# The lead-in moved wholly into the first block of an attention kernel, with low parts subtracted by GpSimd

## The reference

```
q_in = x Wq; Q = [q_in, conv3(q_in)] Wqproj            (K likewise, V = x Wv), 16 heads of 16
tau, delta = sigmoid(pointwise(gelu(depthwise_conv3(x))))   one row per head each
S = Q K^T / 4 * tau[query] + delta[key]; out = softmax(S) V
x = layernorm(x + out Wout)
x = layernorm(x + quantised_linear(x))
```

## Time and profile before

| what | us |
|---|---|
| median of 3 runs (lowest, highest) | 1694.66 (1692.73, 1697.91) |
| the profiled execution | 1700.33 |
| its span | 1698.5 |
| TensorE busy (share of the span) | 1642.5 (97%) |
| VectorE busy | 1538.2 (91%) |
| ScalarE busy | 1322.7 (78%) |
| GpSimd busy | 74.6 (4%) |
| its mean granted clock of TensorE, as a share of full | 0.981 |

### The profile page before, as it was taken

How to read it: one execution, slowest core, us unless ns; L and a number is a source line. 1 busy time by engine, 2 the same in 40 slices (tenths; PEclk the granted TensorE clock), 3 DMA queues, 4 the chain that set the end, 5 groups by cost and what they waited for, 6 DMA issues and landing times.

```text
span 1698.5 us, 33654 instructions
## 1 busy us (share of the span) xinstructions
PE 1642.5 (97%) x13972; PEld 745.1 (44%) x13978; DVE 1538.2 (91%) x1638; ACT 1322.7 (78%) x2389; POOL 74.6 (4%) x133
## 2 busy tenths in 40 slices
PE   8999989999999999999999999999999999998977
PEld 7677754333333333333333333333333333334466
DVE  5588977999999999999999999999999999985797
ACT  3688723888888888888888888888888888885534
POOL 3000003000000000000000000000000000001110
PEclk9899997999999999999999999999999999999998
DMA  3376436000600060006002400322050000002232
GB/s 111 91 191 171 123 91 95 9 8 8 76 16 8 8 84 8 8 9 83 8 14 30 66 8 8 51 44 61 29 71 21 8 8 8 8 8 86 82 101 75
DMA packets 46961, 84.73 MB, mean 50 GB/s; under 512 B 9116, under 2 KB 21020, under 8 KB 44092
## 3 DMA queue, kind: packets, MB, share of 16 engines
q1 hardware_dynamic: 44952, 82.49, 22.6%
q10 hardware_dynamic: 1856, 0.09, 0.1%
HBM read 51.36 MB, written 30.67 MB: 48 GB/s over the span
## 4 chain that ended last, share of the span: by engine, by line
PE 62%; DVE 21%; ACT 1%; issue 1%; ACTq 0%; POOL 0%; DVEq 0%
PE ps L846 26%; PE ps L833 20%; DVE mx L218 17%; PE ps L208 11%; PE ps L869 1%; PE ps L914 1%; PE ps L867 1%; PE ps L820 0%; DVE stats L1059 0%; DVE work L1094 0%; DVE work L1093 0%; ACT e L989 0%; DVE work L1085 0%; DVE small L1080 0%; DVE scr L1089 0%
## 5 line engine op out<-in xcount | busy, mean ns | idle before, releaser
L218 DVE TENSOR_REDUCE mx<-ps 128x2 f32<-128x1024 f32 x1024 | 1230.4, 1223 | 60.6 <-PE ps L208 51.2
L989 ACT ACTIVATE e<-ps 128x512 f32<-128x512 f32 x2048 | 1110.3, 596 | 210.5 <-PE ps L833 170.4
L846 PE MATMUL ps<-e,v_grp 128*32 128x256 f32 x8192 | 657.7, 393 | 0.2 <-issue 0.2
L833 PE MATMUL ps<-q,k 52*128 52x512 f32 x2048 | 525.3, 499 | 4.0 <-ACT e L989 4.0
L208 PE MATMUL ps<-k,q 50*128 50x512 f32 x2048 | 420.8, 404 | 11.1 <-DVE mx L218 6.5
L833 PEld LDWEIGHTS ps<-q,k 52*128 52x128 f32 x2048 | 199.4, 184 | 430.8 <-ACT e L989 400.0
L846 PEld LDWEIGHTS ps<-e,v_grp 128*32 128x32 f32 x8192 | 162.1, 108 | 359.2 <-issue 202.4
L208 PEld LDWEIGHTS ps<-k,q 50*128 50x128 f32 x2048 | 198.9, 188 | 39.7 <-DVE mx L218 31.0
L608 PE MATMUL ps<-x_p,m_p 128*128 128x512 f32 x576 | 143.1, 405 | 0.0
L608 PEld LDWEIGHTS ps<-x_p,m_p 128*128 128x128 f32 x576 | 109.1, 193 | 31.0 <-issue 6.5
L440 DVE SCALAR_TENSOR_TENSOR hid<-x_c,dw_w,hid 128x512 f32<-128x512 f32 x128 | 88.5, 746 | 13.2 <-ACT hid L382 13.2
(11 more groups left out here) (127 smaller groups left out, 621.8 us busy)
## 6 DMA issues: line engine op xcount, KB each, us to landing
k<-k_parts SPq DMA_DIRECT2D x42, 256.0 KB
q<-q_parts SPq DMA_DIRECT2D x42, 256.0 KB
k_parts<-k_sp SPq DMA_DIRECT2D x16, 512.0 KB, 5.1
q_parts<-q_sp SPq DMA_DIRECT2D x16, 512.0 KB, 4.6
att<-ev SPq DMA_DIRECT2D x32, 256.0 KB
x_c<-in_x_t SPq DMA_DIRECT2D x8, 514.0 KB, 6.4
tau_r<-tau_rows SPq DMA_DIRECT2D x16, 256.0 KB
x_in<-in_x SPq DMA_DIRECT2D x8, 512.0 KB, 3.7
```

The lines of the kernel that those rows point to most:

```text
L218: nc.vector.tensor_reduce(mx[:, j % 2, :, jh, qt, kc], ps[:, b0:b0 + 2, :], AX.X, ALU.max).then_inc(s_free, 1)
L833: nc.tensor.matmul(ps[:, st_bank(n), :], k_set[r, g % 2, jh, kt * P:(kt + 1) * P], q_set[r, g % 2, jh, lo:lo + CH], start=True, stop=True) ...
L846: last = nc.tensor.matmul(ps[32 * h:32 * (h + 1), 0, PVW * part:PVW * (part + 1)], v_grp[:, kt, h, :], e[:, x % E_BUFS, h * CH + PVW * par ...
L989: nc.scalar.activation(e[:, x % E_BUFS, h * CH:(h + 1) * CH], ps[:, st_bank(n), :], ACT.Exp).then_inc(e_ready, 1)
```

## The change

The lead-in at the start of the second block goes, with its unused products. The first block now issues 42 items in steps 2 to 7 over 15 places in a step, some of them inside a projection (after products 6, 12 and 18). The loop begins with item 42 in place of 45. Query block 0 takes its units by key chunk, so that a unit only needs the chunks loaded so far. The row maxima of query block 0 are split, transposed and stored in step 7. The low parts of x, delta and q are subtracted by GpSimd. The second half of the values of chunk 0 goes to bank 5. ScalarE's table for the exponential is loaded by an extra instruction at the end of the first block. SyncE waits for the stores of k, q and delta at the start of the second block, and for the group load before the one that it issues.

```diff
-        lead_in = items.index((1, LEAD))
+        def place_of(j, u):
+            if j == 0:
+                return u % (HH * TT) // HH, u % HH, u // (HH * TT)
+            return u // (HH * NQ), u // NQ % HH, u % NQ
 ...
+            qt, jh, kc = place_of(j, u)
+            if j == 0 and (qt, jh) == (0, 0):
+                pe.wait_ge(group_loaded, 16 * GROUP_DMAS * (kc + 1))
+            if u == 0 and j % NQ == 0 and j > 0:
                 pe.wait_ge(group_loaded, loads_of(g + 1))
 ...
-        V_BANK, TD_BANK = 2, 3
+        v_bank = lambda n, v: 5 if (n, v) == (0, 1) else 2
+        TD_BANK = 3
-        PRE_STEP = {4: (0, 0, 0, 0, 0, 0, 2), 5: (0, 0, 1, 1, 1, 1, 1), 6: (0, 0, 1, 1, 1, 1, 1), 7: (2, 2, 2, 2, 2, 2, 4)}
+        ONE_EACH = lambda *places: [int(p in places) for p in range(15)]
+        PRE_STEP = {2: ONE_EACH(6, 9, 10, 13, 14)} | {n: ONE_EACH(5, 6, 9, 10, 13, 14) for n in range(3, 7)} | {7: [1] * 13 + [0, 0]}
+        DVE_PLACES = ((0, 1, 2), (3, 4, 5), (6,), (7, 8, 9), (10,), (11, 12, 13), (14,))
 ...
+                        if n > 1:
+                            sp.wait_ge(group_loaded, 16 * GROUP_DMAS * (n - 1))
                         group_load(sp, 0, group_loaded, slice((n - 1) * CH, n * CH))
 ...
+                    if n == NCHUNK - 1:
+                        rows_store(sp, 0)
 ...
+                def split_low(n):
+                    pool.wait_ge(x_high, n + 1)
+                    low(nc.gpsimd, x_p[:, n % 2, 1], x_c[:, n % 2], x_p[:, n % 2, 0]).then_inc(x_ready, 1)
+                    pool.wait_ge(x_ready, n + 1)
 ...
+                for n in range(NCHUNK):
+                    if n + 1 < NCHUNK:
+                        split_low(n + 1)
+                    if n == NCHUNK - 1:
+                        split_max(pool, 0)
+                        pool.wait_ge(nm_ready, 1)
+                    pool.wait_ge(d_high, n + 1)
+                    low(nc.gpsimd, d_sp[32:32 + H, 1], td[32:32 + H], d_sp[32:32 + H, 0]).then_inc(d_split, 1)
+                    pool.wait_ge(d_split, n + 1)
+                    for o in range(CT):
+                        pool.wait_ge(q_high, CT * n + o + 1)
+                        low(nc.gpsimd, q_sp[:, o, 1], qx[:, o], q_sp[:, o, 0]).then_inc(q_split, 1)
+                        pool.wait_ge(q_split, CT * n + o + 1)
 ...
+                nc.scalar.activation(warm_exp[:], eps_col[:], ACT.Exp)
 ...
+                        if m % 6 == 5:
+                            pre_scores(n, place + m // 6)
 ...
-                    for s in range(PRE, lead_in):
-                        s_item(s)
-                        for m in range(WARM):
-                            for half in range(2):
-                                r = rows_of(half, K_S)
-                                nc.tensor.matmul(ps[:, st_bank(half), :], q_set[r, 0, 0, 0:P], k_set[r, 0, 0, 0:CH], start=True, stop=True)
 ...
-                    issued = lead_in
+                    issued = PRE
```

More of the change, by code:

```diff
@@ L189, in layer_kernel @@
         s_bank = lambda s: 4 + 2 * (s % 2)
+        warm_exp = sb(top, "warm_exp", [P, 1])
+        nm = sb(top, "nm", [P, HG * TT])
+        nm_pad = sb(top, "nm_pad", [P, P], F32R)
+        nm_parts = nm_pad[:, 0:2 * HG * TT].rearrange("p (h t q) -> p h t q", h=HG, t=2)
+        nm_rows = sb(top, "nm_rows", [2 * HG * TT, P], F32R)
+        nm_max, nm_high, pad_zero, rows_set = sem("nm_max"), sem("nm_high"), sem("pad_zero"), sem("rows_set")
+        ROWS_INC = 16 * HG
         mx = sb(top, "mx", [P, 2, 2, HH, TT, NQ])
@@ L215, in max_unit, with rows_turn, rows_copy, row_maxima @@
             dve.wait_ge(s_full, s + 1)
-            qt, jh, kc = u // (HH * NQ), u // NQ % HH, u % NQ
+            qt, jh, kc = place_of(j, u)
             b0 = s_bank(s)
             nc.vector.tensor_reduce(mx[:, j % 2, :, jh, qt, kc], ps[:, b0:b0 + 2, :], AX.X, ALU.max).then_inc(s_free, 1)
+        def rows_turn(pe, s):
+            j, u = items[s]
+            pe.wait_ge(s_free, s - 1)
+            pe.wait_ge(nm_ready, j + 1)
+            nc.tensor.transpose(ps[:, s_bank(s), 0:P], nm_pad[:].bitcast(F32), ident_f[:]).then_inc(s_full, 1)
+        def rows_copy(dve, s):
+            j, u = items[s]
+            dve.wait_ge(s_full, s + 1)
+            if j > 0:
+                dve.wait_ge(rows_set, j * ROWS_INC)
+            nc.vector.tensor_copy(nm_rows[:], ps[0:2 * HG * TT, s_bank(s), 0:P]).then_inc(s_free, 1)
+        def row_maxima(dve, s):
+            j, u = items[s]
+            dve.wait_ge(s_free, s + 1)
+            if j > 0:
+                dve.wait_ge(nm_ready, j)
+            nc.vector.tensor_reduce(nm[:], mx[:, j % 2].rearrange("p a j q c -> p (a j q) c"), AX.X, ALU.max, negate=True).then_inc(nm_max, 1)
+        def split_max(pool, j):
+            pool.wait_ge(nm_max, j + 1)
+            if j > 0:
+                pool.wait_ge(s_full, rows_at[j - 1] + 1)
+            cols = nm[:].rearrange("p (h q) -> p h q", h=HG)
+            high(nc.gpsimd, nm_parts[:, :, 0], cols).then_inc(nm_high, 1)
+            pool.wait_ge(nm_high, j + 1)
+            low(nc.gpsimd, nm_parts[:, :, 1], cols, nm_parts[:, :, 0]).then_inc(nm_ready, 1)
+        def rows_store(sp, j):
+            sp.wait_ge(s_free, rows_at[j] + 1)
+            g, lo = j // NQ, j % NQ * CH
+            for h in range(HG):
+                row = HALF * (h // HH) + ROW_MAX
+                sp.dma_start(q_set[row:row + 2, g % 2, h % HH, lo:lo + CH].bitcast(F32).rearrange("t (a l) -> t a l", a=TT),
+                             nm_rows[h * 2 * TT:(h + 1) * 2 * TT, :].bitcast(F32)).then_inc(rows_set, 16)
         early = top.enter_context(ExitStack())
+        q_sp = sb(early, "q_sp", [P, CT, 2, CH], F32R)
+        k_sp = sb(early, "k_sp", [P, CT, 2, CH], F32R)
+        td = sb(early, "td", [48, CH])
+        d_sp = sb(early, "d_sp", [48, 2, CH], F32R)
         x_c = sb(early, "x_c", [P, 2, CT, CH + TAPS - 1])
@@ L532, in pre_max @@
                 def pre_max(n, place):
-                    for s in pre_at.get((n, place), ()):
+                    for s in (s for p in DVE_PLACES[place] for s in pre_at.get((n, p), ())):
+                        j, u = items[s]
+                        if u == "rows":
+                            rows_copy(dve, s)
+                            continue
                         max_unit(dve, s)
+                        if u == UNITS - 1:
+                            row_maxima(dve, s)
                 for n in range(NCHUNK):
@@ L633, in pre_scores @@
                     for s in pre_at.get((n, place), ()):
-                        s_unit(pe, s)
+                        if items[s][1] == "rows":
+                            rows_turn(pe, s)
+                        else:
+                            s_unit(pe, s)
                 beta(1, 0)
@@ L785, in layer_kernel @@
             PVW = CH // 2
-            WARM = 3
             st_bank = lambda n: 1 + n % ST_BUFS
[L791 to L798, removed]
             with nc.Block() as block:
```

98 lines of the change are left out of this document (26 added, 72 removed).

## The result

| | us |
|---|---|
| before, median of 4 runs (lowest, highest) | 1696.29 (1692.73, 1705.17) |
| after, median of 4 runs (lowest, highest) | 1926.8 (1918.15, 1935.2) |
| ratio, 95% interval | 1.1346 [1.1296, 1.1395] |
| span of the profiled execution, before and after | 1698.5, 1916.4 |
| mean granted clock, before and after | 0.981, 0.891 |

Slower, as forecast, but by 13.5% and not 7.4%: 1926.8 lies outside 1740 to 1900.

What follows compares the result with a forecast made beforehand. TensorE was taken to set the pace in the first block and the loop. Terms -15.6 + 69 + 70 + 2 = +125 on the profiled 1700.3 us gave 1826, so 1820 against the median 1694.7; range 1740 to 1900.

Steps and rivals of the forecast that it cites:

- Lead-in and warm-up products, -15.6: Boundary of first and second block: loop's value products start at 264 instead of 279.6, -15.6 us (-12 to -18).
- The 1.1 us taken off in step 0: First block, step 0: bank 5 and the moved subtraction of x save 1.1 us (0 to 2.0).
- Subtractions on GpSimd, 0: First block: subtractions moved to GpSimd cost 0 us, upper end +12 from VectorE standing still beside them.
- Rival 4: First block: VectorE becomes the bound through GpSimd, +12 us; with rival 3 1693 us, chance 0.04.
- Rows three items late, +69: Loop: TensorE waits for row maxima, 2.05 us in 24 blocks and 3.3 in six, +69 us (64 to 82).
- The clock in the loop, +70: Loop: 12 clock falls behind the waits at 5.8 us each, +70 us (0 to 174).
- rival 2: Loop: clock falls in nearly every block, 139 us instead of 70; 1890 us, up to 1925; chance 0.14.
- rival 1: Loop: the waits stay but the clock does not fall; 1750 us, chance 0.20.
- Block 30, +2: Block 30: TensorE's wait for its rows grows by 1.2 us, three more items cost a little; +2 us (0 to 3).
- Rival 3: Loop: the wait is caught up in the 28 slots after it, so it ends faster; 1681 us, chance 0.12.

Runs made afterwards that it cites:

- experiment 7: Kernel of experiment 2 (change, 45 items ahead of the loop) with the low parts of x, deltas and q subtracted on VectorE again: 1694.51 us, ratio 0.9972.
- experiment 5: Kernel before the change with LEAD 10 instead of 12, nothing else: 1791.53 us, ratio 1.0561.
- experiment 3: Changed kernel with unused products ahead of the key tile that waits for the rows, 10 pairs a block (15 in blocks 24 to 29): 1777.61 us, ratio 1.0468.
- experiment 1: Kernel before the change with LEAD 9 instead of 12, none of the first block's edits: 1929.2 us, ratio 1.1321.
- experiment 4: Changed kernel with DEFER 1 instead of 3, the rows item two units earlier, still 42 items: 1705.21 us, ratio 1.0032.
- experiment 2: Changed kernel with 45 items issued in the first block instead of 42, so the lead is restored: 1695.16 us, ratio 0.9984.
- experiment 6: Kernel before the change with LEAD 11 instead of 12, nothing else: 1709.96 us, ratio 1.0066.
- experiment 8: Kernel of experiment 2 with unused products at the boundary, 16 pairs, then 3 after each of the first four key-tile calls: 1690.79 us, ratio 0.9951.

## Why the prediction was wrong, by its own steps

**Lead-in and warm-up products, -15.6: nearly right.** Steps took 26.12 and 26.83 (26.1 and 26.7 predicted), the boundary's idle is 3.81 us, the first key tile came at 262.49 (261.5) and the first value product at 266.63 (265, then 264). The gain is 13.0 us at this product and 14.1 at the end of query block 0 (310.73 against 324.85). The 1.1 us taken off in step 0 did not come. The first eight taps and the pointwise products behind the GELU, in the change and in experiment 7:

```profile
57.65 8.01 DVE L519 SCALAR_TENSOR_TENSOR hid<-x_c,dw_w,hid 128x512 f32<-128x512 f32 x8
67.91 6.71 PE L702 MATMUL ps<-hid,pw_w 128*16 128x512 f32 x16 [4.88 <-ACT hid L466]
...
62.74 5.38 DVE L501 SCALAR_TENSOR_TENSOR hid<-x_c,dw_w,hid 128x512 f32<-128x512 f32 x8
71.51 6.18 PE L698 MATMUL ps<-hid,pw_w 128*16 128x512 f32 x16 [3.00 <-ACT hid L448]
```

From the first tap to the pointwise products it takes 10.26 us beside GpSimd and 8.77 without it. TensorE waits for the GELU either way, 3.00 us even without GpSimd, and 1.5 us longer with it.

**Subtractions on GpSimd, 0: right within some 6 us**, which is what experiment 7 can tell. Their contention is real and hidden under TensorE in the later steps, but not in step 0 (the 1.5 us above). Rival 4 fell.

**Rows three items late, +69: mechanism right, term somewhat small.** 79.0 us. The way was 4.43 us and not 4.1, so the waits were 2.3 and 3.5 rather than 2.05 and 3.3. The choice between 3.9 and 4.5 was the error: the row read 4.53 with the DMA as last releaser, and I took less because the idle ahead of it looked usual. With 4.43 the sum would have been 24 x (4.43 - 2.05) + 6 x (4.43 - 0.8) = 79. The estimate of 4.6 from the Trainium skill, "DMA: Bandwidth & Descriptors", section on the anatomy of one DMA, was nearer than mine; but that section describes a DMA issued by GpSimd, and these are issued by SyncE, so the nearness is no test of it.

**The clock in the loop, +70: the step that failed.** It took 12 falls of 5.8 us; there were 27 in the change, at (226.3 - 79.0) / 27 = 5.5 each, where 226.3 is by how much the stretch from the copy of query block 1's row maxima (in block 0) to that of query block 31's (in block 30) grew. The price of one fall, 5.8 from the stretch in the earlier trace rows, came out right on the mean, with luck: that one stretch was 13.7 us long, and in the change they run from 3.4 to 27.3. Their number was wrong. I had two rows, 1.48 us with no fall and 3.58 with one, and drew a line between them. The row of 1.48 comes from the last query block, where no score units stand between the products any more (whether that is why the clock stayed up isn't shown); in the middle of the loop experiment 5 has low stretches after waits of 1.38 to 1.74 us. What happened is rival 2, held at 0.14. That its upper end of 1925 is 2 us from the result is in part luck: it has 30 x 5.8 = 174 for the clock where 147 was measured, and 69 for the waits where 79 was. Experiment 3 gives nearly the same for this term from other runs, 149 us.

The Trainium skill, "TensorE: Matmul & The Clock Gate", section "Why this matters for your kernels", has only longer gaps drop the clock; here waits of 2.3 us did in nearly every block, so the measurement decides against using it for a loop like this one. I had cited it in favour of rival 1, which fell with the result: 1750 needs a clock that stays.

**Block 30, +2: the wait right, the clock behind it left out.** The block takes 52.2 us against 46.65, 5.5 more. The waits there, in the change and before:

```profile
PE ps L238 <- POOL nm_pad L87: 2.2, 1, 2.2
...
PE ps L820 <- POOL nm_pad L87: 1.2, 1, 1.2
```

So the wait grew by 1.0 us (1.2 predicted), and 10.2 us of low clock follow it, which the kernel before doesn't have there. At 1 - 1.24 / 2.16 of the low time that is some 4.3 us, an estimate. A fall of the clock was priced for the waits for the rows and not for this one.

**Rival 3** (the wait is caught up) is refuted: where the clock stayed up, the block is 42.64, which is 40.26 and the whole wait.

With the measured sizes the sum closes on the profiled spans: -14.1 to the end of query block 0, + 229.1 from there to the end of query block 31 (79.0 of it waits for the rows, 147 the clock behind them, 5.5 in block 30, and 2.7 less in the last block), + 2.9 behind it = 217.9 = 1916.4 - 1698.5.

What stays open: what decides that one wait of 2.3 us brings a fall and another doesn't, and why a low stretch lasts 3.4 us once and 27.3 another time. And whether the way itself could be cut (fewer or parallel transfers for the rows) wasn't tried.

## What to carry to other kernels

When work is moved ahead of a loop, count the items: what is missing at the start shifts everything that the dealing-out order places, here a handover that had 4.53 - 4.43 = 0.1 us of slack in six blocks, and one slot (1.24 us) more in the others. Price a new wait on TensorE twice, once as the wait and once as the clock after it: here 79 us of waits came with 147 us of slow products. Where a wait can't be avoided, products whose results nobody uses keep the clock up: they turned 1926.8 us into 1777.6 with the rows as late as ever.

## What the runs showed of the hardware that was not expected

- In a stream of products that otherwise has no gap, idle times of 2.3 us and more for the rows were followed by a granted clock of 0.50 in 61 of 66 cases (the change and experiments 1 and 5), 2.22 us in block 30 in 4 of 4 (the change, experiments 1, 3 and 4), 1.38 to 1.74 us in 6 of 6 (experiments 3, 4 and 5), 1.22 us in block 30 in 3 of 6 (experiments 2, 6 and 7, but not the kernel before, 5 and 8), and 1.04 to 1.10 for the rows in 0 of 31 (experiments 4, 5 and 6); yet an idle time of 1.05 us at 608.40 in experiment 8 was followed by 20.5 us of low clock. After waits for the rows, the low stretches last from 3.4 to 27.3 us.
- So the loss is steep in the lateness: leads of 12, 11, 10 and 9 give 1699, 1710, 1792 and 1929 us, with waits of 0, 8, 41 and 79.
- VectorE's tap on two tensors in SBUF stands nearly still while GpSimd subtracts on two others: 2.90 us for the tap beside a subtraction of 2.51, 1.77 beside one of 1.61, 0.74 alone. GpSimd is held up a little as well: its subtraction on 16 partitions x 512 takes 1.61 us beside taps and 1.28 in step 7, where there are none. That is as long as one on 128 partitions x 512 takes, 1.28.
